# Layer-norm sums S1 to S4 moved from VectorE to GpSimd in a two-layer graph network kernel

## The chip, the cores and the metric

The kernel runs on one core of one Trainium2 chip. Five engines work side by side on it: TensorE (PE, matrix products), VectorE (DVE, elementwise), ScalarE (ACT, activations and copies), GpSimd (POOL, elementwise, slower) and SyncE (SP, which here issues DMAs). The metric is the device time of one execution in microseconds (us); the time before is 1575.23 us, the median of 3 runs (1575.11 to 1575.33).

## What is computed

```
# layer 0
h = relu(layernorm(x))                      # x: (16, 1024, 128)
x = x + (adj @ (h @ W0) + b0)               # adj: (1024, 1024)
# layer 1, five gated steps
h = relu(layernorm(x))
repeat 5 times:
    m  = adj @ h ; av = [m, m]
    z  = sigmoid(av @ w3.T + w3_b + h @ u3.T + u3_b)
    r  = sigmoid(av @ w4.T + w4_b + h @ u3.T + u3_b)
    hv = tanh(av @ w5.T + w5_b + (r * h) @ u5.T + u5_b)
    h  = (1 - z) * h + z * hv
x = x + h
```

## The kernel before

The 16 batches go in 4 groups `p` of 4 batches, each group in two slots of 2 batches. A group takes two layer rounds (`layer(p, slot)`: adj times the normalised x, layer 0) and ten step rounds (`step(p, t, slot)`: the five gated steps of layer 1). `all_rounds` gives the order, the same on every engine: the layer rounds of group p+1 are put among the last step rounds of group p, and the two slots alternate, so that TensorE works on one slot while the other engines finish the other.

adj times h is done by a Strassen-like scheme of seven half-size products (K_A0, K_S1, K_S2, K_A1, K_S3, K_B1, K_S4) with fp16 high and low parts, so each product is 12 matmuls of 128x512. Four of the seven need sums of the quarters of h. For the state inside a step they are made by `sum_state` on VectorE. For a layer norm's output they are the subject here:

- `moments` (L322 to L349, GpSimd): 18 small instructions on 128x16 that turn the statistics into `rstd` and `shift`.
- `normalise` (L810, ScalarE): writes the normalised rows into the one buffer `ysc`, 4 quarters of 4 blocks.
- `round_n` part 0 and 1 (L826, ScalarE) and `rest_n` part 0 and 1 (L1190, VectorE): the fp16 high and low parts of the four plain quarters.
- `sum_n` (L1201, L1202, L1205, L1207, VectorE): four adds and subtractions of 128x512 fp32 that overwrite `ysc` by S1 to S4. They wait for the low parts 0 and 1 of `rest_n`, since those read what is overwritten. Its `parts` let the caller put two of the four in each of two places.
- `round_n` and `rest_n` part 2 and 3: the high and low parts of S1 to S4. Part 2 (S1, S2) waits for the third of the four instructions, part 3 for the fourth. K_S1 to K_S4 of TensorE wait for these.

There are 16 such layer norms: (p, layer, slot). Layer 0 of a group is normalised while the group before still steps; layer 1 between the group's layer rounds and its first steps. Each engine executes its instructions strictly in the order in which its function writes them; semaphores (`wait_ge`) tie the engines together. What comes just behind the sums matters in three places: `new_state` (L1232, L1236, L1238, VectorE) makes the new h of the other slot, whose completion (`h_ready`) ScalarE's `evacuate` (L850) waits for, and TensorE cannot open the bank of K_S2 before that evacuation. `output` (L1284) adds the result to x.

The two lines that decide who waits for a sum:

```
act.wait_ge(n_sum_done[layer], 4 * n + part + 1)   # round_n, part 2 and 3
pool.wait_ge / dve.wait_ge(n_lo_done[layer], 4 * n + 2)   # first sum
```

Of the kernel before, what the change touches and what calls it, by code (L numbers as in the profile page):

```python
# [5 lines left out]
def gnn_kernel(nc, x, adj, w0, b0, w3, b3, u3, c3, w4, b4, w5, b5, u5, c5, out):  # L6
# [13 lines left out]
    END = STEPS - 1  # L20
# [42 lines left out]
    with ctx:  # L63
# [70 lines left out]
        ysc = sb("ysc", [P, 2 * BLOCKS, D])  # L134
# [149 lines left out]
        def n_layer(p, slot):  # L284
            return 2 * p + slot
# [199 lines left out]
        @block.gpsimd  # L485
        def _(pool):
            pool.memset(ones[:, :], 1.0)
            pool.memset(ident[:, :], 0.0).then_inc(ident_done, 1)
            pool.wait_ge(ident_done, 1)
            pool.affine_select(out=ident[:, :], in_=ident[:, :], compare_op=ALU.not_equal, fill=1.0, base=0,  # L490
                               pattern=[[-1, P]], channel_multiplier=1).then_inc(ident_done, 1)

            def scale_weights():


                pool.wait_ge(top_ready, 1)
                pool.wait_ge(w_maxed, 1)
                nc.gpsimd.tensor_scalar(w_max[:, 3:5], w_max[:, 3:5], 1.0 / SCALE16, None, ALU.mult)
                nc.gpsimd.tensor_scalar(w_max[:, 0:3], w_max[:, 0:3], m_inv[:, :], 1.0, ALU.mult, ALU.mult
                                        ).then_inc(w_op, 1)  # L500
                pool.wait_ge(w_op, 1)
                nc.gpsimd.tensor_scalar(w_max[:, 1:2], w_max[:, 1:2], w_max[:, 0:1], None, ALU.max)
                nc.gpsimd.tensor_scalar(w_max[:, 2:3], w_max[:, 2:3], w_max[:, 4:5], None, ALU.max
                                        ).then_inc(w_op, 1)
                pool.wait_ge(w_op, 2)
                nc.gpsimd.tensor_scalar(w_max[:, 1:2], w_max[:, 1:2], w_max[:, 3:4], None, ALU.max).then_inc(w_op, 1)
                pool.wait_ge(w_op, 3)
                nc.gpsimd.tensor_scalar(w_exp[:, :], w_max[:, 1:3].bitcast(I32), 1.0 / EXP_UNIT, LEAST_EXP,
                                        ALU.mult, ALU.max).then_inc(w_op, 1)
                pool.wait_ge(w_op, 4)  # L510
                nc.gpsimd.tensor_scalar(w_scale[:, :].bitcast(I32), w_exp[:, :], -EXP_UNIT,
                                        (254 + TOP_EXP) * EXP_UNIT, ALU.mult, ALU.add)
                nc.gpsimd.tensor_scalar(w_inv[:, :].bitcast(I32), w_exp[:, :], EXP_UNIT, -TOP_EXP * EXP_UNIT,
                                        ALU.mult, ALU.add).then_inc(w_op, 1)
                pool.wait_ge(w_op, 5)
                for w, by, also in ((WZR, GATES, m_inv[:, :]), (WR, GATES, m_inv[:, :]), (WV, CAND, m_inv[:, :]),
                                    (UZR, GATES, 1.0 / SCALE16), (UV, CAND, 1.0 / SCALE16)):
                    last = nc.gpsimd.tensor_scalar(w_raw[:, w, :], w_raw[:, w, :], w_scale[:, by:by + 1], also,
                                                   ALU.mult, ALU.mult)
                last.then_inc(w_scaled, 1)  # L520

            for slot in range(2):
                moments(pool, 0, 0, slot)
            scale_weights()
            for slot in range(2):
                moments(pool, 0, 1, slot)
            for p in range(1, GROUPS):
                for layer in range(2):
                    for slot in range(2):
                        moments(pool, p, layer, slot)  # L530

        @block.tensor
        def _(pe):
# [520 lines left out]
        def _(dve):  # L1054
# [135 lines left out]
                nc.vector.tensor_sub(lo8[:, at[1], :], rows4[:, at[0], :], hi8[:, at[1], :]  # L1190
                                     ).then_inc(n_lo_done[layer], 1)

            def sum_n(p, layer, slot, parts=range(2)):

                n, done = n_layer(p, slot), n_sum_done[layer]
                a0, a1, b0_, b1 = (flat(quarter(ysc, q)) for q in range(4))
                if 0 in parts:
                    dve.wait_ge(n_lo_done[layer], 4 * n + 2)
                    if layer == 0:
                        dve.wait_ge(y_ready[0], 4 * n + 4)  # L1200
                    nc.vector.tensor_add(b1, b0_, b1).then_inc(done, 1)  # L1201
                    nc.vector.tensor_sub(b0_, a0, b0_).then_inc(done, 1)  # L1202
                if 1 in parts:
                    dve.wait_ge(done, 4 * n + 1)
                    nc.vector.tensor_sub(a0, b1, a0).then_inc(done, 1)  # L1205
                    dve.wait_ge(done, 4 * n + 3)
                    nc.vector.tensor_sub(a1, a1, a0).then_inc(done, 1)  # L1207

            def first_h(p, slot):
                for k in range(2):  # L1210
                    part = (slice(None), slice(2 * k, 2 * k + 2), slice(None))
# [75 lines left out]
            def layer(p, slot):  # L1287
                g = g_layer(p, slot)
                if p == 0 and slot == 0:
# [5 lines left out]
                    rest_n(0, 0, 0, 0)  # L1295
                    rest_n(0, 0, 0, 1)
                    rest_rows(K_A1)
                    sum_n(0, 0, 0)
                    sum_rows(K_S2)
                    rest_rows(K_S4)  # L1300
                    rest_n(0, 0, 0, 2)
# [14 lines left out]
                    rest_m(g, 3)  # L1316
                    rest_m(g, 2)
                    rest_n(0, 0, 1, 1)
                    sum_n(0, 0, 1)
                    sum_m(g, 1, START_ORDER)  # L1320
                    rest_n(0, 0, 1, 2)
                    rest_m(g, 1)
# [3 lines left out]
                elif p == 0:  # L1326
# [8 lines left out]
                    rest_m(g, 2)  # L1335
                    sum_m(g, 1, LAYER_ORDER)
                    rest_m(g, 1)
                    sum_n(0, 1, 0)
                    rest_n(0, 1, 0, 2)
                else:  # L1340
                    t, other = (END, 0) if slot == 1 else (END - 1, 1)
# [27 lines left out]
            def step(p, t, slot):  # L1369
# [39 lines left out]
                if sums:  # L1409
                    rest_s(e, 1)  # L1410
                rest_m(g, 3)
                if steps_ahead(p, t, slot, END, 0):
                    sum_n(p + 1, 0, 1, [0])
                rest_m(g, 2)
                if t == 0:
                    dve.wait_ge(h_first_done, 2 * n_layer(p, slot) + 2)
# [7 lines left out]
                sum_m(g, 1)  # L1424
                rest_rh(s, 3)
                rest_m(g, 1)
                if steps_ahead(p, t, slot, END, 0):
                    sum_n(p + 1, 0, 1, [1])
                if steps_ahead(p, t, slot, 3, 0):
                    rest_n(p + 1, 0, 0, 0)  # L1430
                if steps_ahead(p, t, slot, END, 1):
                    rest_n(p + 1, 1, 0, 1)
                    sum_n(p + 1, 1, 0, [0])
                if steps_ahead(p, t, slot, 3, 1):
                    sum_n(p + 1, 0, 0, [1])
                times_h(s, slot, 2)
                if first0 and p > 0:
                    rest_n(p, 1, 1, 1)
                times_h(s, slot, 1)
                rest_rh(s, 2)  # L1440
                if first0 and p > 0:
                    sum_n(p, 1, 1, [0])
                rest_rh(s, 1)
                if first0 and p > 0:
                    sum_n(p, 1, 1, [1])
                if steps_ahead(p, t, slot, END, 1):
                    sum_n(p + 1, 1, 0, [1])
                    rest_n(p + 1, 1, 0, 2)
                    rest_n(p + 1, 1, 0, 3)
                if steps_ahead(p, t, slot, 1, 1):  # L1450
# [2 lines left out]
                    statistics0(p + 1, 1)  # L1453
                if steps_ahead(p, t, slot, 3, 0):
                    rest_n(p + 1, 0, 0, 1)
                    sum_n(p + 1, 0, 0, [0])
                if steps_ahead(p, t, slot, 3, 1):
                    rest_n(p + 1, 0, 0, 2)
                    rest_n(p + 1, 0, 0, 3)
# [8 lines left out]
                if first0 and p == 0:  # L1468
                    rest_n(p, 1, 1, 0)
                    rest_n(p, 1, 1, 1)  # L1470
                    sum_n(p, 1, 1)

            all_rounds(layer, step)
            s, n = n_step(GROUPS - 1, END, 1), n_layer(GROUPS - 1, 1)
# [31 lines left out]
```

## Time and profile before

| | |
|---|---|
| median of 3 runs | 1575.23 us |
| the profiled execution | 1574.88 us |
| its span, first to last instruction | 1573.1 us |
| TensorE busy | 1464.5 us, 93% |
| VectorE busy | 1256.9 us, 80% |
| ScalarE busy | 948.5 us, 60% |
| GpSimd busy | 169.8 us, 11% |
| mean granted TensorE clock | 0.976 of full speed (2.4 GHz) |

The profile is of one execution. Between the span and the execution's own time lie 1.8 us of launch and end. A row of a timeline has the start, the duration, the engine, the line, the operation and the shapes; in brackets stands how long the engine was idle before and what released it. "x2" is two instructions merged in one row. TensorE's matmuls overlap, so that a row of one shows 0.38 us while twelve take 2.59 us.

### The profile page before, as it was taken

What the parts mean: (1) busy time and instruction counts of PE and PEld (TensorE: products, weight loads), DVE (VectorE), ACT (ScalarE), POOL (GpSimd) and SP (SyncE); (2) the same over time, 40 slices, a digit from 0 to 9 for tenths busy, and PEclk for the clock granted to TensorE, in tenths of its full rate; (3) what the DMA queues carried; (4) which work ended last, traced back from release to release, by engine and by line L of the source; (5) the groups of instructions that cost most, each with busy time, mean ns of one, the idle gap of its engine ahead of it and who ended that gap; (6) DMA issues with size and microseconds to landing.
All of it is one profiled execution on the core that took longest, in us unless ns stands there. A gap on an engine that the chain in (4) does not pass through costs nothing.

```text
span 1573.1 us, 19899 instructions
## 1 busy us (share of the span) xinstructions
PE 1464.5 (93%) x6951; PEld 673.5 (43%) x6951; DVE 1256.9 (80%) x1697; ACT 948.5 (60%) x1470; POOL 169.8 (11%) x388
## 2 busy tenths in 40 slices
PE   4778999999998899999998999999999889999997
PEld 3433444444443344444443434444444334444443
DVE  8866888888857978988877878888885787887777
ACT  5536566766546665676564755676664656556653
POOL 1212004400210001500101000440021000000000
PEclk9889999999999999999999999999999999999998
DMA  4011334321213243333212234422221323333322
GB/s 177 1 27 27 78 61 94 58 54 41 48 31 78 57 91 101 57 69 62 38 24 67 57 75 87 94 57 54 41 48 31 77 54 64 78 57 64 67 49 80
DMA packets 316625, 97.42 MB, mean 62 GB/s; under 512 B 310256, under 2 KB 311152, under 8 KB 316528
## 3 DMA queue, kind: packets, MB, share of 16 engines
q1 hardware_dynamic: 314800, 95.49, 28.3%
q8 instruction: 57, 0.93, 0.3%
q10 hardware_dynamic: 1728, 0.66, 0.2%
q14 instruction: 40, 0.33, 0.1%
HBM read 13.24 MB, written 8.39 MB: 14 GB/s over the span
## 4 chain that ended last, share of the span: by engine, by line
PE 77%; DVE 12%; ACT 5%; issue 4%; POOL 1%; DMA 1%; ACTq 0%; SPq 0%; DVEq 0%; POOLq 0%
PE ps_a L562 29%; PE ps_c L562 13%; PE ps_b L562 7%; PE ps_u L618 6%; PE ps_u L622 6%; PE ps_u L620 6%; PE ps_v L620 4%; PE ps_v L622 4%; PE ps_v L618 4%; DVE nx_lo L1190 2%; ACT ysc L810 1%; DVE t_lo L1111 1%; ACT nx_hi L826 1%; DVE rh L1236 1%; DVE area L1238 1%
## 5 line engine op out<-in xcount | busy, mean ns | idle before, releaser
L562 PE MATMUL ps_a<-t_hi,nx_hi 128*128 128x512 f16 x640 | 248.8, 389 | 47.1 <-ACT rh L850 19.8
L562 PE MATMUL ps_a<-t_lo,nx_hi 128*128 128x512 f16 x640 | 248.6, 388 | 0.0
L562 PE MATMUL ps_a<-t_hi,nx_lo 128*128 128x512 f16 x640 | 248.1, 388 | 0.0
L850 ACT ACTIVATE rh<-ps_a 128x512 f32<-128x512 f32 x144 | 85.1, 591 | 197.7 <-PE ps_a L562 161.1
L863 ACT ACTIVATE rh<-ps_v,bias,w_inv 128x512 f32<-128x512 f32 x160 | 123.8, 776 | 93.0 <-PE ps_v L622 93.0
L1271 DVE TENSOR_TENSOR rh<-rh,area 128x512 f32<-128x512 f32 x160 | 108.9, 691 | 65.8 <-ACT rh L868 62.0
L859 ACT ACTIVATE m_hi<-rh 128x512 f16<-128x512 f32 x144 | 90.1, 627 | 112.2 <-DVE rh L1221 111.7
L1226 DVE SCALAR_TENSOR_TENSOR m_lo<-rh,m_hi 128x512 f16<-128x512 f32 x144 | 99.0, 691 | 56.7 <-ACT m_hi L859 51.3
L1232 DVE SCALAR_TENSOR_TENSOR rh<-rh,area 128x1024 f32<-128x1024 f32 x80 | 97.8, 1222 | 44.7 <-ACT rh L863 44.3
L876 ACT ACTIVATE area<-ps_u,bias,w_inv 128x512 f32<-128x512 f32 x160 | 122.4, 771 | 17.2 <-PE ps_u L622 16.9
L868 ACT ACTIVATE rh<-ps_u,bias,w_inv 128x512 f32<-128x512 f32 x160 | 120.0, 774 | 17.6 <-PE ps_u L622 16.0
L1275 DVE TENSOR_TENSOR rh_lo<-rh,rh_hi 128x512 f16<-128x512 f32 x160 | 110.0, 687 | 25.0 <-ACT rh_hi L881 23.4
L322 POOL TENSOR_TENSOR mean<-stats 128x16 f32<-128x16 f32 x16 | 15.8, 988 | 1008.0 <-DVE stats L1149 516.3
L618 PE MATMUL ps_u<-m_hi,w_hi 128*128 128x512 f16 x320 | 121.5, 380 | 0.4
L622 PE MATMUL ps_u<-m_hi,w_lo 128*128 128x512 f16 x320 | 121.5, 380 | 0.0
L620 PE MATMUL ps_u<-m_lo,w_hi 128*128 128x512 f16 x320 | 121.5, 380 | 0.0
L562 PE MATMUL ps_c<-t_lo,nx_hi 128*128 128x512 f16 x320 | 121.3, 379 | 0.0
L562 PE MATMUL ps_c<-t_hi,nx_lo 128*128 128x512 f16 x320 | 121.3, 379 | 0.0
L562 PE MATMUL ps_c<-t_hi,nx_hi 128*128 128x512 f16 x320 | 121.3, 379 | 0.0
L562 PEld LDWEIGHTS ps_a<-t_hi,nx_hi 128*128 128x128 f16 x640 | 63.6, 99 | 131.6 <-issue 25.8
L830 ACT ACTIVATE h_hi<-area 128x1024 f16<-128x1024 f32 x78 | 82.2, 1054 | 58.6 <-DVE area L1238 58.6
L1236 DVE TENSOR_TENSOR rh<-rh,area 128x1024 f32<-128x1024 f32 x80 | 98.3, 1228 | 8.7 <-DVE rh L1232 0.5
(180 smaller groups left out, 3053.3 us busy)
## 6 DMA issues: line engine op xcount, KB each, us to landing
xr<-in_x_dram SPq DMA_DIRECT2D x6, 1024.0 KB, 5.1
out_dram<-xr SPq DMA_DIRECT2D x6, 1024.0 KB, 4.0
area<-in_adj_dram SPq DMA_DIRECT2D x8, 512.0 KB, 8.3
nx_hi<-s SPq DMA_TRANSPOSE x128, 2.4
nx_lo<-s SPq DMA_TRANSPOSE x128, 2.5
area<-in_x_dram SPq DMA_DIRECT2D x2, 1024.0 KB, 5.1
nx_hi<-h_hi SPq DMA_TRANSPOSE x96, 2.4
nx_lo<-h_lo SPq DMA_TRANSPOSE x96, 2.5
```

The costliest lines, as they stand in the source:

```text
L562: last = nc.tensor.matmul(o[:, :], a[:, PLACE[k], j, :], b[:, k, j, :], start=(opens and j == 0 and n == 0), stop=(j == HB - 1 and n == 2) ...
L618: nc.tensor.matmul(bank_out[:, :], w_hi[:, w, :], a_hi[:, q, :], start=start, stop=False, skip_group_check=reopen)
L620: nc.tensor.matmul(bank_out[:, :], w_hi[:, w, :], a_lo[:, q, :], start=False, stop=False, skip_group_check=reopen)
L622: return nc.tensor.matmul(bank_out[:, :], w_lo[:, w, :], a_hi[:, q, :], start=False, stop=stop, skip_group_check=reopen)
L863: nc.scalar.activation(cand[:, q, :], V_BANK[q][:, :], ACT.Tanh, bias=bias[:, BV:BV + 1], scale=w_inv[:, CAND:CAND + 1]).then_inc(cand_rea ...
L868: nc.scalar.activation(rh[:, q, :], U_BANK[q][:, :], ACT.Sigmoid, bias=bias[:, BR:BR + 1], scale=w_inv[:, GATES:GATES + 1]).then_inc(r_rea ...
L876: nc.scalar.activation(z[:, q, :], U_BANK[q][:, :], ACT.Sigmoid, bias=bias[:, BZ:BZ + 1], scale=w_inv[:, GATES:GATES + 1]).then_inc(z_read ...
L1226: nc.vector.scalar_tensor_tensor(out=m_lo[:, q, :], in0=source, scalar=M_SCALE, in1=m_hi[:, q, :], op0=ALU.mult, op1=ALU.subtract).then_in ...
L1232: nc.vector.scalar_tensor_tensor(out=cand[part], in0=cand[part], scalar=SCALE16, in1=h[slot][part], op0=ALU.mult, op1=ALU.subtract).then_i ...
L1236: nc.vector.tensor_mul(cand[part], cand[part], z[part]).then_inc(zdiff_done, 1)
L1271: nc.vector.tensor_mul(rh[:, q, :], rh[:, q, :], h[slot][:, q, :]).then_inc(rh_done, 1)
L1275: nc.vector.tensor_sub(rh_lo[:, q, :], rh[:, q, :], rh_hi[:, q, :]).then_inc(rh_lo_done, 1)
```

## The change

`sum_n` is taken out of VectorE's program with all its calls, and written as a function of GpSimd's, with the same four instructions, waits and semaphore counts. GpSimd calls it between its `moments`: right behind the moments of the same norm at the start (group 0), and in the groups 1 to 3 as follows: the moments of both slots of layer 0, the sums (0, slot 0), the moments (1, slot 0), the sums (0, slot 1), the moments (1, slot 1), and then the sums of layer 1 of both slots. The split of the four instructions over two places is gone. TensorE's, ScalarE's and SyncE's programs stay as they are.

```diff
@@ gpsimd
-            for slot in range(2):
-                moments(pool, 0, 0, slot)
+            def sum_n(p, layer, slot):
+
+                n, done = n_layer(p, slot), n_sum_done[layer]
+                a0, a1, b0_, b1 = (flat(quarter(ysc, q)) for q in range(4))
+                pool.wait_ge(n_lo_done[layer], 4 * n + 2)
+                if layer == 0:
+                    pool.wait_ge(y_ready[0], 4 * n + 4)
+                nc.gpsimd.tensor_add(b1, b0_, b1).then_inc(done, 1)
+                nc.gpsimd.tensor_sub(b0_, a0, b0_).then_inc(done, 1)
+                pool.wait_ge(done, 4 * n + 1)
+                nc.gpsimd.tensor_sub(a0, b1, a0).then_inc(done, 1)
+                pool.wait_ge(done, 4 * n + 3)
+                nc.gpsimd.tensor_sub(a1, a1, a0).then_inc(done, 1)
+
+            moments(pool, 0, 0, 0)
+            sum_n(0, 0, 0)
+            moments(pool, 0, 0, 1)
             scale_weights()
-            for slot in range(2):
-                moments(pool, 0, 1, slot)
+            sum_n(0, 0, 1)
+            moments(pool, 0, 1, 0)
+            sum_n(0, 1, 0)
+            moments(pool, 0, 1, 1)
+            sum_n(0, 1, 1)
             for p in range(1, GROUPS):
-                for layer in range(2):
-                    for slot in range(2):
-                        moments(pool, p, layer, slot)
+                for slot in range(2):
+                    moments(pool, p, 0, slot)
+                sum_n(p, 0, 0)
+                moments(pool, p, 1, 0)
+                sum_n(p, 0, 1)
+                moments(pool, p, 1, 1)
+                for slot in range(2):
+                    sum_n(p, 1, slot)
@@ vector
-            def sum_n(p, layer, slot, parts=range(2)):
...
@@ vector, the calls (each removed)
-                if steps_ahead(p, t, slot, END, 0):
-                    sum_n(p + 1, 0, 1, [0])
...
-                    sum_n(p + 1, 1, 0, [0])
...
-                    sum_n(p, 1, 1)
```

What moves is shown by the order of the instructions at two places. The first is GpSimd in group 1, behind the moments of layer 1, slot 1 (L345 to L349 end the moments, `ysc` is the buffer of the sums). Before:

```order
L345 TENSOR_SCALAR newton<-newton 128x16
L347 TENSOR_TENSOR rstd<-rstd,newton 128x16
L349 TENSOR_TENSOR shift<-mean,rstd 128x16
L322 TENSOR_TENSOR mean<-stats 128x16
L323 TENSOR_TENSOR gap<-stats 128x16
```

And now:

```order
L345 TENSOR_SCALAR newton<-newton 128x16
L347 TENSOR_TENSOR rstd<-rstd,newton 128x16
L349 TENSOR_TENSOR shift<-mean,rstd 128x16
L529 TENSOR_TENSOR ysc<-ysc 128x512
L530 TENSOR_TENSOR ysc<-ysc 128x512
L532 TENSOR_TENSOR ysc<-ysc 128x512
L534 TENSOR_TENSOR ysc<-ysc 128x512
L529 TENSOR_TENSOR ysc<-ysc 128x512
L530 TENSOR_TENSOR ysc<-ysc 128x512
L532 TENSOR_TENSOR ysc<-ysc 128x512
L534 TENSOR_TENSOR ysc<-ysc 128x512
```

Eight large instructions stand behind the last moments of the group, those of slot 0 and of slot 1.

The second is VectorE in the first step round of group 1, where the sums of layer 1, slot 1 were (`nx_lo` are the low parts, `rh` the product of r and h, L1232 begins the new state). Before:

```order
L1271 TENSOR_TENSOR rh<-rh,area 128x512
L1190 TENSOR_TENSOR nx_lo<-ysc,nx_hi 128x1024
L1271 TENSOR_TENSOR rh<-rh,area 128x512
L1275 TENSOR_TENSOR rh_lo<-rh,rh_hi 128x512
L1201 TENSOR_TENSOR ysc<-ysc 128x512
L1202 TENSOR_TENSOR ysc<-ysc 128x512
L1275 TENSOR_TENSOR rh_lo<-rh,rh_hi 128x512
L1205 TENSOR_TENSOR ysc<-ysc 128x512
L1207 TENSOR_TENSOR ysc<-ysc 128x512
L1190 TENSOR_TENSOR nx_lo<-ysc,nx_hi 128x2x512
L1232 SCALAR_TENSOR_TENSOR rh<-rh,area 128x2x512
```

And now (the same functions, 23 lines further down until the removed `sum_n`, 7 behind it):

```order
L1278 TENSOR_TENSOR rh<-rh,area 128x512
L1213 TENSOR_TENSOR nx_lo<-ysc,nx_hi 128x1024
L1278 TENSOR_TENSOR rh<-rh,area 128x512
L1282 TENSOR_TENSOR rh_lo<-rh,rh_hi 128x512 x2
L1213 TENSOR_TENSOR nx_lo<-ysc,nx_hi 128x2x512
L1239 SCALAR_TENSOR_TENSOR rh<-rh,area 128x2x512
```

The four rows on `ysc` are gone; the low part of S1 and S2 still stands in front of the new state.

## Rows read from the trace of the kernel before

**Rows 1.** Page, part 1: busy time of each engine.
```profile
PE 1464.5 (93%) x6951; PEld 673.5 (43%) x6951; DVE 1256.9 (80%) x1697; ACT 948.5 (60%) x1470; POOL 169.8 (11%) x388
```

**Rows 2.** Page, part 4: the chain that ended last, by engine.
```profile
PE 77%; DVE 12%; ACT 5%; issue 4%; POOL 1%; DMA 1%; ACTq 0%; SPq 0%; DVEq 0%; POOLq 0%
```

**Rows 3.** Waits of TensorE: waiter, releaser, us in total, times, longest.
```profile
PE ps_a L562 <- DVE nx_lo L1190: 18.2, 5, 3.7
PE ps_a L562 <- DVE ny_lo L1190: 8.5, 3, 2.8
```

**Rows 4.** Tile ysc: one of the four sums; min/median/max ns.
```profile
L1201 DVE TENSOR_TENSOR ysc<-ysc x16: 683/692/707, 30.1 to 1267.8; 128x512 f32<-128x512 f32 x16
```

**Rows 5.** GpSimd's groups by shape: count, busy us, mean ns.
```profile
L518 POOL TENSOR_SCALAR nx_hi<-nx_hi,w_scale,m_inv 128x128 f32<-128x128 f32 x3 | 1.3, 451 | 0.1
L518 POOL TENSOR_SCALAR nx_hi<-nx_hi,w_scale 128x128 f32<-128x128 f32 x2 | 0.7, 370 | 0.0
```

**Rows 6.** Timeline, GpSimd beside VectorE, then (457.99) GpSimd alone.
```profile
281.52 1.26 DVE L1236 TENSOR_TENSOR rh<-rh,area 128x1024 f32<-128x1024 f32 x1
...
281.66 1.21 POOL L324 TENSOR_TENSOR var_eps<-stats 128x16 f32<-128x16 f32 x1
...
457.99 0.23 POOL L324 TENSOR_TENSOR var_eps<-stats 128x16 f32<-128x16 f32 x1
```

**Rows 7.** Timeline 339 to 348 us: sums of group 1, layer 0, slot 0.
```profile
339.28 0.69 DVE L1190 TENSOR_TENSOR ny_lo<-ysc,ny_hi 128x512 f16<-128x512 f32 x1
...
341.41 1.23 DVE L1232 SCALAR_TENSOR_TENSOR rh<-rh,area 128x1024 f32<-128x1024 f32 x1
...
344.00 1.22 DVE L1238 TENSOR_TENSOR area<-area,rh 128x1024 f32<-128x1024 f32 x1
...
345.79 0.59 ACT L850 ACTIVATE rh<-ps_a 128x512 f32<-128x512 f32 x1
...
347.50 0.38 PE L562 MATMUL ps_a<-t_hi,nx_hi 128*128 128x512 f16 x1
```

**Rows 8.** Timeline 415 to 423 us: group 1, layer 0, slot 1.
```profile
415.97 0.69 POOL L349 TENSOR_TENSOR shift<-mean,rstd 128x16 f32<-128x16 f32 x1
...
421.60 1.04 ACT L826 ACTIVATE ny_hi<-ysc 128x1024 f16<-128x1024 f32 x1
```

**Rows 9.** Timeline 474 to 482 us: group 1, layer 1, slot 0.
```profile
474.34 1.22 DVE L1190 TENSOR_TENSOR nx_lo<-ysc,nx_hi 128x1024 f16<-128x1024 f32 x1
...
480.70 1.06 ACT L826 ACTIVATE nx_hi<-ysc 128x1024 f16<-128x1024 f32 x1 [1.36 <-DVE ysc L1205]
```

**Rows 10.** Timeline 517 to 525 us: group 1, layer 1, slot 1.
```profile
517.32 1.23 DVE L1190 TENSOR_TENSOR nx_lo<-ysc,nx_hi 128x1024 f16<-128x1024 f32 x1 [0.25 <-ACT nx_hi L826]
...
522.46 1.05 ACT L826 ACTIVATE nx_hi<-ysc 128x1024 f16<-128x1024 f32 x1
...
523.55 1.23 DVE L1190 TENSOR_TENSOR nx_lo<-ysc,nx_hi 128x1024 f16<-128x1024 f32 x1 [0.46 <-ACT nx_hi L826]
```

**Rows 11.** Timeline 25 to 35 us: group 0, layer 0, slot 0.
```profile
25.73 1.83 DVE L1190 TENSOR_TENSOR ny_lo<-ysc,ny_hi 128x1024 f16<-128x1024 f32 x2
...
32.64 2.28 DVE L1098 TENSOR_TENSOR s<-area 128x2048 f32<-128x2048 f32 x1
```

**Rows 12.** Timeline 70 to 75 us: group 0, layer 0, slot 1.
```profile
70.74 0.68 DVE L1190 TENSOR_TENSOR ny_lo<-ysc,ny_hi 128x512 f16<-128x512 f32 x1
...
73.39 1.06 ACT L826 ACTIVATE ny_hi<-ysc 128x1024 f16<-128x1024 f32 x1 [2.77 <-DVE ysc L1205]
```

**Rows 13.** Timeline 101 to 111 us: group 0, layer 1, slot 0.
```profile
101.89 2.36 DVE L1190 TENSOR_TENSOR nx_lo<-ysc,nx_hi 128x1024 f16<-128x1024 f32 x2 [8.36 <-ACT nx_hi L826]
...
108.68 2.00 ACT L826 ACTIVATE nx_hi<-ysc 128x1024 f16<-128x1024 f32 x2 [2.56 <-DVE ysc L1205]
```

**Rows 14.** Timeline 146 to 152 us: group 0, layer 1, slot 1.
```profile
146.00 2.36 DVE L1190 TENSOR_TENSOR nx_lo<-ysc,nx_hi 128x1024 f16<-128x1024 f32 x2 [1.58 <-ACT nx_hi L826]
...
150.32 1.06 ACT L826 ACTIVATE nx_hi<-ysc 128x1024 f16<-128x1024 f32 x1 [2.74 <-DVE ysc L1205]
```

More of the change, by code:

```diff
@@ L1191, in rest_n @@
                                      ).then_inc(n_lo_done[layer], 1)
-            def sum_n(p, layer, slot, parts=range(2)):
[L1195 to L1207, printed above, removed]
             def first_h(p, slot):
@@ L1297, in layer @@
                     rest_rows(K_A1)
-                    sum_n(0, 0, 0)
                     sum_rows(K_S2)
@@ L1318, in layer @@
                     rest_n(0, 0, 1, 1)
-                    sum_n(0, 0, 1)
                     sum_m(g, 1, START_ORDER)
@@ L1337, in layer @@
                     rest_m(g, 1)
-                    sum_n(0, 1, 0)
                     rest_n(0, 1, 0, 2)
@@ L1426, in step @@
                 rest_m(g, 1)
-                if steps_ahead(p, t, slot, END, 0):
-                    sum_n(p + 1, 0, 1, [1])
                 if steps_ahead(p, t, slot, 3, 0):
@@ L1432, in step @@
                     rest_n(p + 1, 1, 0, 1)
-                    sum_n(p + 1, 1, 0, [0])
-                if steps_ahead(p, t, slot, 3, 1):
-                    sum_n(p + 1, 0, 0, [1])
                 times_h(s, slot, 2)
@@ L1440, in step @@
                 rest_rh(s, 2)
-                if first0 and p > 0:
-                    sum_n(p, 1, 1, [0])
                 rest_rh(s, 1)
-                if first0 and p > 0:
-                    sum_n(p, 1, 1, [1])
                 if steps_ahead(p, t, slot, END, 1):
-                    sum_n(p + 1, 1, 0, [1])
                     rest_n(p + 1, 1, 0, 2)
@@ L1455, in step @@
                     rest_n(p + 1, 0, 0, 1)
-                    sum_n(p + 1, 0, 0, [0])
                 if steps_ahead(p, t, slot, 3, 1):
```

## Prediction

> **What bounds the kernel now.** I read the busy times first, then the chain of work that ended last, then who TensorE waited for, then the 16 places of the sums one by one. TensorE is busy for 93% of the span, VectorE for 80%, GpSimd for 11% [rows 1]: GpSimd has room, and VectorE is not the bound on average. The chain agrees: 77% of it lies on TensorE, 12% on VectorE, 5% on ScalarE [rows 2]. So 64 instructions less on VectorE are worth nothing where TensorE runs on. They matter where TensorE waits, and there the rows name layer-norm low parts: 18.2 us in 5 waits for `nx_lo` and 8.5 us in 3 waits for `ny_lo` [rows 3]. These stand behind the sums in the dependences (copy of S1 and S2, then low part, then on VectorE the new state). What counts is therefore not the time that a sum takes of an engine, but when its third instruction ends, and what it keeps VectorE from.
>
> **What is removed.** 64 sums of 0.69 us [rows 4], at most 44 us of VectorE in all, 2.8 us per norm. Waits, matmuls, copies and DMAs are as before; no DMA moves past another queue.
>
> **What is added: the price of a sum on GpSimd.** The trace has none of this size. GpSimd's nearest rows are scalings of 128x128, 0.44 us each in the form with two pointers (1.3 us for 3) and 0.36 with one (0.7 us for 2) [rows 5], against 0.23 us for a 128x16 instruction alone [rows 6]. The slopes are 0.13/112 = 1.2 ns and 0.21/112 = 1.9 ns per element; 496 elements more give 0.8 and 1.15 us. In proportion to elements alone the dear form gives 4 x 0.44 = 1.75 us. A sum reads two tensors, so I take the dearer form's slope, 1.15 us, and keep 0.8 and 1.75 as ends. The Trainium skill (GPSIMD Engine Reference, "Performance versus the Vector engine") measures 4497 ns for a two-input add of 2048 elements, an estimate of about 1.12 us for 512, by which the sum below would be the same.
>
> **What the two engines do to each other.** A 128x16 instruction on GpSimd takes 0.23 us alone but 1.21 us when it starts 0.14 us behind VectorE's L1236, and it ends 0.09 us after that one's end (281.66 + 1.21 = 282.87 against 281.52 + 1.26 = 282.78) [rows 6]. So GpSimd waits for the end of a VectorE instruction with two SBUF inputs. For the other direction the rows show only a trace: that L1236 takes 1.26 us, where its like of the same size, L1232, takes 1.23 [rows 6, 7]. A sum has 32 times the elements of that GpSimd instruction, 32 x 0.03 = 1.0 us: I take it that VectorE stands still for about 1.05 us per sum whenever it wants to start an instruction with two SBUF inputs meanwhile, and that they then take turns. The ends are 0 (nothing held) and 1.75 (the sum's whole length at its dear price). The Trainium skill (SBUF — State Buffer, "Who interferes with whom") says that the two share a read port, exclusively and for a whole instruction. Taken literally it makes the hold the full length of the sum, 1.15 us, and would add 0.1 us to each hold.
>
> **Group 0 (all four norms lie on the chain).**
> - Layer 0, slot 0: GpSimd can begin when the low parts end, 27.56. VectorE next does high and low parts of adj out of PSUM, which read one SBUF tensor, and then L1098, which before began at 32.64 behind the sums [rows 11] and could now where the first sum began, 30.1 [rows 4]. GpSimd's third sum holds it to about 31.1. VectorE has no idle time from there until the next norm's statistics: -1.5.
> - Layer 0, slot 1: the low part ends at 71.42, three sums later it is 71.42 + 3 x 1.15 + 0.1 = 74.97; ScalarE's copy, which waits for them, began at 73.39 [rows 12] and everything queued behind it goes with it: +1.55.
> - Layer 1, slot 0: from 104.25 three sums end at 107.8, or 108.4 with one VectorE instruction in between, against 108.68 [rows 13]: -0.3.
> - Layer 1, slot 1: from 148.36, ready at 151.9 against 150.32 [rows 14]; nothing else is left for VectorE to do there: +1.55.
>
> Together +1.3 us.
>
> **Groups 1 to 3 (three times the same picture, 374 us apart).**
> - Layer 0, slot 0: the low part ends at 339.97, and GpSimd runs its four sums from there, long before the copy that needs them. From 341.41 VectorE makes the new state: three dependent instructions with two SBUF inputs each, up to L1238 (344.00) [rows 7]. The second sum has just begun when L1232 wants to start, the third and fourth get in at its two next boundaries: 1.0 + 1.05 + 1.05 = 3.1 us later. Cover: L1238 ended at 345.22, the evacuation L850 began at 345.79 (0.57 us of slack), ended at 346.38, and TensorE needed it at 347.50 (1.12 us) [rows 7]. So TensorE waits 3.1 - 0.57 - 1.12 = 1.4, say 1.5 us with the semaphores, in a stretch where it has no idle time: +1.5. The two sums that VectorE is spared further on give nothing back, for TensorE doesn't wait there.
> - Layer 0, slot 1: GpSimd's moments end at 416.66, and its sums are queued behind them (before, two of them ran on VectorE earlier than that). The third ends at 416.66 + 3 x 1.15 = 420.1 plus two or three turns of VectorE of 0.69, 421.5 or 422.2; the copy began at 421.60 [rows 8]. VectorE's small work shifts by up to 1 us, but TensorE's wait of 2.8 us behind it hangs on a later evacuation and the fourth sum, long ready: 0.
> - Layer 1, slot 0: from 475.56, three sums and three turns of VectorE: 475.56 + 3.45 + 2.07 = 481.08, against 480.70 for a copy that waited 1.36 us for a sum already [rows 9]. What VectorE is spared it spends on being held: +0.4.
> - Layer 1, slot 1: the low part ends at 518.55. Three sums and three turns (one `rh`, two `rh_lo`): 518.55 + 3.45 + 2.07 = 524.07. The copy began at 522.46, its low part at 523.55, and the new state, on which TensorE's 3.7 us wait hangs, directly behind [rows 10, 3]: 524.07 - 522.46 = +1.6.
>
> Together 3.5 us per group, 10.5 for three. Behind the waiting sums on GpSimd stand only moments whose statistics come later than the sums end, so nothing else is held up.
>
> **Sum.** 1.3 + 10.5 = +11.8 us. The profiled execution took 1574.88 us, so 1586.7; the median of the runs is 0.35 above it: 1587.0 us.
>
> **The rivals.**
> 1. *VectorE is not held by GpSimd* (other side). Only GpSimd gives way. Then group 0 comes to -2.5 (L1098 at 30.1 instead of 32.64) + 1.55 - 0.9 (107.8 against 108.68) + 1.55 = -0.3 us; in the later groups the first and last places cost nothing and at 480.70 the copy comes when ScalarE is free, 1.36 us earlier [rows 9]: -1.4 x 3 = -4.2, in all -4.5 us, 1571 us. For it speaks that VectorE's row is longer by 0.03 us only; against it, that it is longer at all. It decides if the hold is under about 0.2 us.
> 2. *Short sums.* At 0.8 to 0.9 us per sum each third sum ends 0.9 us earlier: 3 x 0.9 + 0.3 less in group 0, about 0.75 less in each of the three costly places of the others, 9.8 in all: +2.0 us, 1577 us, which no measurement of this kernel tells from no change (0.2%, 3.2 us, is the bound used below).
> 3. *Long sums*, 1.75 us: 0.6 x 3 = 1.8 us more at each of three places in group 0 and 0.6 at the first, 1.8 more at each of the four of the other groups: 6 + 21.6 more, 1615 us.
> 4. *The change does nothing* is no case: the order of GpSimd and VectorE moves as written, and the ends of the sums move with it.
>
> **How the numbers follow.** The forecast has 0.52, rival 1 0.15, rival 2 0.18, rival 3 0.10; 0.05 is left for a mix that lands near zero or just below. The range 1570 to 1600 takes in the forecast with holds of 0.8 to 1.4 us and rivals 1 and 2, and leaves rival 3 out. Slower by over 0.2%: 0.52 + 0.10 + a little of rival 2 = 0.65; within: 0.18; faster: 0.17.
>
> **What would show it.** Right: GpSimd's sums of 1.1 to 1.2 us alone and 1.7 to 1.9 beside VectorE; L1232 to L1238 of the place at 341 us, or those between them, longer by about 1 us each or started that much later; TensorE idle by 1 to 2 us before K_S2 at 347 us; the copy at 522.46 released by a GpSimd sum. Wrong: VectorE rows of unchanged length beside the sums, or TensorE's waits for `nx_lo` shorter than 18.2 us in all.

## The result and the profile after

| | before | after |
|---|---|---|
| median of the runs (range) | 1575.28 us (1575.11 to 1577.5), 4 runs | 1590.42 us (1589.21 to 1591.99), 4 runs |
| profiled execution | 1574.88 us, span 1573.1 | 1591.56 us, span 1589.8 |
| granted TensorE clock, mean over the span | 0.976 | 0.973 |

The ratio is 1.0096, with a 95% interval of 1.008 to 1.0111: the change costs 15.1 us (12.6 to 17.5). The forecast was 11.8 us.

The page's busy times and its chain by engine, of the changed kernel:

```profile
PE 1473.5 (93%) x6951; PEld 675.3 (42%) x6951; DVE 1255.0 (79%) x1633; ACT 949.2 (60%) x1470; POOL 264.7 (17%) x452
...
PE 75%; DVE 12%; ACT 5%; issue 4%; POOL 3%; DMA 0%; ACTq 0%; SPq 0%; DVEq 0%; POOLq 0%
```

Against [rows 1] VectorE has 64 instructions less, which were 44 us of work [rows 4], and yet is only 1.9 us less busy (1256.9 to 1255.0). The other 42 us came back as longer instructions. GpSimd went from 1% of the chain [rows 2] to 3%.

The four sums on GpSimd, by tile (count, then min/median/max ns, first and last start):

```profile
L529 POOL TENSOR_TENSOR ysc<-ysc x16: 1264/1270/1657, 27.7 to 1282.0; 128x512 f32<-128x512 f32 x16
L530 POOL TENSOR_TENSOR ysc<-ysc x16: 1263/1714/1733, 28.9 to 1283.2; 128x512 f32<-128x512 f32 x16
L532 POOL TENSOR_TENSOR ysc<-ysc x16: 1267/1718/3434, 30.1 to 1284.9; 128x512 f32<-128x512 f32 x16
```

A sum takes 1.27 us when nothing is in its way and mostly 1.72 us beside VectorE; one took 3.43. The prediction had 1.15 alone and expected 1.7 to 1.9 beside VectorE.

VectorE beside GpSimd, in the timeline of group 1 (start us, length us; in brackets the idle time before and its releaser). This is the place of [rows 7], layer 0, slot 0; the kernel's lines have moved, L1232 is L1239, L1236 is L1243, L1238 is L1245, L850 is L873 and L562 is L585:

```profile
344.55 1.27 POOL L529 TENSOR_TENSOR ysc<-ysc 128x512 f32<-128x512 f32 x1 [41.87 <-DVE ny_lo L1213]
345.77 1.27 POOL L530 TENSOR_TENSOR ysc<-ysc 128x512 f32<-128x512 f32 x1
345.92 2.20 DVE L1239 SCALAR_TENSOR_TENSOR rh<-rh,area 128x1024 f32<-128x1024 f32 x1 [1.45 <-ACT rh L886]
347.00 2.25 POOL L532 TENSOR_TENSOR ysc<-ysc 128x512 f32<-128x512 f32 x1
348.22 2.10 DVE L1243 TENSOR_TENSOR rh<-rh,area 128x1024 f32<-128x1024 f32 x1
...
350.36 2.17 DVE L1245 TENSOR_TENSOR area<-area,rh 128x1024 f32<-128x1024 f32 x1
...
353.27 0.39 PE L585 MATMUL ps_a<-t_hi,nx_hi 128*128 128x512 f16 x1 [1.10 <-ACT rh L873]
```

The engines take turns, one instruction each. L1239 starts 0.15 us behind the second sum and needs 1.23 us alone [rows 7]; the sum ends at 345.77 + 1.27 = 347.04, and 347.04 + 1.23 = 348.27 against its end at 348.12, 0.15 us earlier. The third sum, issued at 347.00, ends 1.13 us behind that, at 349.25. Each of the three VectorE instructions is 0.87 to 0.97 us longer than in [rows 7] (L1236 there takes 1.23 us). At the end of them stands a TensorE wait of 1.10 us where none was. The Trainium skill (SBUF — State Buffer, "Who interferes with whom") says that the port pair which VectorE and GpSimd share is an exclusive lock, and that a VectorE instruction with two SBUF inputs contends with a GpSimd instruction that reads SBUF; these rows agree, in both directions.

### The profile page after: what moved, and what is told of

Read it like the earlier page. It is cut to its first block, busy times and chain, and to the rows that moved or that the text cites. A ratio compares the mean times of both kernels' runs of the same rounds, so it can differ in the third digit from the quotient of the medians.

```text
span 1589.8 us, 19899 instructions
## 1 busy us (share of the span) xinstructions
PE 1473.5 (93%) x6951; PEld 675.3 (42%) x6951; DVE 1255.0 (79%) x1633; ACT 949.2 (60%) x1470; POOL 264.7 (17%) x452
## 4 chain that ended last, share of the span: by engine, by line
PE 75%; DVE 12%; ACT 5%; issue 4%; POOL 3%; DMA 0%; ACTq 0%; SPq 0%; DVEq 0%; POOLq 0%
PE ps_a L585 29%; PE ps_c L585 12%; PE ps_b L585 7%; PE ps_u L641 5%; PE ps_u L643 5%; PE ps_u L645 5%; PE ps_v L643 3%; PE ps_v L641 3%; PE ps_v L645 3%; DVE nx_lo L1213 2%; DVE area L1245 1%; DVE rh L1243 1%; DVE rh L1239 1%; ACT nx_hi L849 1%; DVE t_lo L1134 1%
## 5 line engine op out<-in xcount | busy, mean ns | idle before, releaser
L585 PE MATMUL ps_a<-t_hi,nx_hi 128*128 128x512 f16 x640 | 250.3, 391 | 53.6 <-ACT rh L873 28.0
L585 PE MATMUL ps_a<-t_lo,nx_hi 128*128 128x512 f16 x640 | 249.7, 390 | 0.0
L585 PE MATMUL ps_a<-t_hi,nx_lo 128*128 128x512 f16 x640 | 249.4, 390 | 0.0
L873 ACT ACTIVATE rh<-ps_a 128x512 f32<-128x512 f32 x144 | 85.2, 592 | 215.7 <-PE ps_a L585 166.3
L1278 DVE TENSOR_TENSOR rh<-rh,area 128x512 f32<-128x512 f32 x160 | 119.6, 756 | 71.0 <-ACT rh L891 66.4
L1233 DVE SCALAR_TENSOR_TENSOR m_lo<-rh,m_hi 128x512 f16<-128x512 f32 x144 | 102.5, 716 | 59.1 <-ACT m_hi L882 54.1
L1282 DVE TENSOR_TENSOR rh_lo<-rh,rh_hi 128x512 f16<-128x512 f32 x160 | 123.6, 775 | 21.7 <-ACT rh_hi L904 20.4
L1239 DVE SCALAR_TENSOR_TENSOR rh<-rh,area 128x1024 f32<-128x1024 f32 x80 | 100.6, 1258 | 45.3 <-ACT rh L886 45.1
L585 PEld LDWEIGHTS ps_a<-t_hi,nx_hi 128*128 128x128 f16 x640 | 63.9, 100 | 140.0 <-ACT rh L873 34.4
L585 PE MATMUL ps_c<-t_hi,nx_hi 128*128 128x512 f16 x320 | 121.3, 379 | 0.7 <-DVE nx_lo L1213 0.7
L585 PE MATMUL ps_c<-t_hi,nx_lo 128*128 128x512 f16 x320 | 121.3, 379 | 0.0
L585 PE MATMUL ps_c<-t_lo,nx_hi 128*128 128x512 f16 x320 | 121.3, 379 | 0.0
L1243 DVE TENSOR_TENSOR rh<-rh,area 128x1024 f32<-128x1024 f32 x80 | 100.9, 1261 | 8.3
```

The costliest lines, as they stand in the source:

```text
L585: last = nc.tensor.matmul(o[:, :], a[:, PLACE[k], j, :], b[:, k, j, :], start=(opens and j == 0 and n == 0), stop=(j == HB - 1 and n == 2) ...
L1233: nc.vector.scalar_tensor_tensor(out=m_lo[:, q, :], in0=source, scalar=M_SCALE, in1=m_hi[:, q, :], op0=ALU.mult, op1=ALU.subtract).then_in ...
L1239: nc.vector.scalar_tensor_tensor(out=cand[part], in0=cand[part], scalar=SCALE16, in1=h[slot][part], op0=ALU.mult, op1=ALU.subtract).then_i ...
L1243: nc.vector.tensor_mul(cand[part], cand[part], z[part]).then_inc(zdiff_done, 1)
L1278: nc.vector.tensor_mul(rh[:, q, :], rh[:, q, :], h[slot][:, q, :]).then_inc(rh_done, 1)
L1282: nc.vector.tensor_sub(rh_lo[:, q, :], rh[:, q, :], rh_hi[:, q, :]).then_inc(rh_lo_done, 1)
```

## Where the time went

TensorE's waits for the same three releasers, of the changed kernel (us in total, times, longest). Before, the first was 19.8 us in 10 waits, the others are [rows 3]:

```profile
PE ps_a L585 <- ACT rh L873: 28.0, 13, 5.5
PE ps_a L585 <- DVE nx_lo L1213: 18.5, 5, 3.7
PE ps_a L585 <- DVE ny_lo L1213: 8.5, 3, 2.8
...
PE ps_u L641 <- DVE m_lo L1233: 1.3, 3, 0.4
```

The waits for low parts, 26.7 us before and 27.0 now, did not change. Three new ones of 1.1 us (layer 0, slot 0), three grown from 0.38 to 1.56 (layer 1, slot 1) and three of 0.44 us for `m_lo` (layer 0, slot 1) make 3 x (1.10 + 1.18 + 0.44) = 8.2 us for groups 1 to 3. Of the first row another 1.4 us belong to group 0: experiment 10, which changes that group alone, has 21.2 us there.

That is not the whole of it. I split each span in three by 2 us windows of TensorE's rows: idle time; time lost to a low clock while busy (busy time x (1 - granted clock), full being 2.4 GHz and 0.50 being 1.2 GHz); and the rest, work at full speed. The last two together are the page's busy time: 1464.5 us before and 1473.5 after, for the same 6951 matmuls.

| profiled execution | span | TensorE idle | lost to low clock | work at full speed |
|---|---|---|---|---|
| before | 1573.1 | 108.6 | 24.8 | 1439.7 |
| after | 1589.8 | 116.3 | 32.7 | 1440.8 |
| difference | +16.7 | +7.7 | +7.9 | +1.1 |

About half of the 16.7 us is clock. The clearest place is behind group 0. Both kernels wait 3.72 us there for a low part; the matmul behind the wait, before and after:

```profile
166.17 0.38 PE L562 MATMUL ps_a<-t_hi,nx_hi 128*128 128x512 f16 x1 [3.72 <-DVE nx_lo L1190]
```

```profile
167.77 0.59 PE L585 MATMUL ps_a<-t_hi,nx_hi 128*128 128x512 f16 x1 [3.72 <-DVE nx_lo L1213]
```

And TensorE in the windows behind it (window, its length, TensorE's busy us with its matmuls, granted clock, DMA share, GB/s), before:

```profile
168.00:170.00 2.00, 2.00 (x11) 1.00 0.00 0
170.00:172.00 2.00, 2.00 (x11) 1.00 0.32 66
```

After:

```profile
168.00:170.00 2.00, 2.00 (x6) 0.50 0.03 8
170.00:172.00 2.00, 2.00 (x7) 0.50 0.00 0
172.00:174.00 2.00, 2.00 (x7) 0.58 0.32 66
```

After a wait of the same length the old kernel went on at full clock and the new one at half for 6 us, which costs 2 x 0.50 x 2 + 2 x 0.42 = 2.8 us, more than any two of the new waits. The same happened behind the waits at 545.6 and 821.9 us (before, 538.3 and 810.7), 1.6 and 1.7 us. The second of them is a wait of 2.82 us in both kernels; after:

```profile
821.91 0.38 PE L585 MATMUL ps_a<-t_hi,ny_hi 128*128 128x512 f16 x1 [2.82 <-DVE ny_lo L1213]
...
822.00:824.00 2.00, 2.00 (x6) 0.55 0.00 0
```

In groups 1 to 3 no low stretch stands behind one of the new waits. In the profiles of both kernels and of every experiment they lie (taken as 2 us windows with a granted clock under 0.95) at three old waits of each group: the one of 3.7 us where the group before ends, the one of 2.8 us some 275 us later, and the one of 5.5 us some 330 us later. At the third the clock fell every time. Behind the other two it fell at 3 of 6 places before and at 6 of 6 after.

Group by group, from the starts of the same matmuls before and after:

| matmul before | after | difference | forecast at that point |
|---|---|---|---|
| 64.74 | 62.16 | -2.6 | -1.5 |
| 104.91 | 104.38 | -0.5 | about 0 |
| 166.17 (end of group 0) | 167.77 | +1.6 | +1.3 |
| 538.31 (end of group 1) | 545.63 | +7.3 | +4.8 |
| 910.15 (end of group 2) | 924.17 | +14.0 | +8.3 |
| 1286.21 (end of group 3) | 1302.90 | +16.7 | +11.8 |

The same groups with idle time and low clock apart, beside two experiments told below that leave the program of groups 1 to 3 as it was (length, in brackets idle / lost to low clock, us):

| | before | experiment 1 | experiment 10 | after |
|---|---|---|---|---|
| group 0 | 166.2 (51.8 / 9.0) | 165.1 (49.8 / 9.8) | 168.2 (51.0 / 11.6) | 167.8 (51.4 / 11.3) |
| group 1 | 372.1 (14.5 / 3.8) | 375.5 (14.5 / 7.4) | 373.2 (14.5 / 5.0) | 377.9 (17.3 / 6.4) |
| group 2 | 371.8 (15.3 / 2.5) | 376.1 (15.3 / 6.6) | 371.9 (15.3 / 2.4) | 378.5 (18.2 / 5.7) |
| group 3 | 376.1 (15.7 / 6.2) | 371.8 (15.3 / 2.6) | 371.9 (15.3 / 2.6) | 378.7 (18.2 / 5.9) |

The new waits of groups 1 to 3 are all there: idle time grows by 8.2 us, as counted above. But a group whose program and waits are the same takes anything from 371.8 to 376.1 us, by the clock: its idle time differs by 0.4 us at most. The kernel before has one such dear group in its profile, the changed one has three.

## The experiments

Two theories stood at the start, here with the letters that the expectations give them. **A**: GpSimd's two-input sums and VectorE's two-input instructions exclude each other, the time is the waits that this makes, and it adds up place by place. **C**: VectorE is not held, only GpSimd gives way; the time comes from sums that are late in themselves. The expectations also weigh **B**: any sum on GpSimd costs, wherever it stands. As the clock rows came in, **D** was added: beside its waits the change makes TensorE's clock fall more often.

All kernels start from the one before. In most of them a set says which sums go to GpSimd, each at the place in GpSimd's order that the change gives it; the others stay on VectorE as before:

```diff
+    ON_POOL = {(0, 0, 0)}          (group, layer, slot)
@@ sum_n of GpSimd (the added one) @@
+                if (p, layer, slot) not in ON_POOL:
+                    return
@@ sum_n of VectorE (the old one) @@
+                if (p, layer, slot) in ON_POOL:
+                    return
```

**1. Only the first norm** (`ON_POOL = {(0, 0, 0)}`).

> Only the very first norm's sums (group 0, layer 0, slot 0) are made by GpSimd, the other 15 stay on VectorE. Theory A (a sum costs by when its third instruction ends and by what it holds up on VectorE): this is the one place of the 16 where it gains, since VectorE is dense there and most of its neighbours read PSUM; TensorE's product at 64.7 us starts 2.5 us earlier (62.2 in the changed kernel) and the time falls by 2 to 3 us. Theory B (any sum on GpSimd costs): slower by 1 us or more. The adj-row sum L1098 starts at 30.1 instead of 32.6 by A.

Measured: 1574.58 us (12 runs, 1569.73 to 1578.38) against 1576.18 (19 runs), ratio 0.9987 with 0.9973 to 1.0001. In the profile TensorE's idle time is 2.5 us less, 106.1. The place of [rows 11]:

```profile
30.31 3.44 POOL L535 TENSOR_TENSOR ysc<-ysc 128x512 f32<-128x512 f32 x1
...
30.33 2.28 DVE L1124 TENSOR_TENSOR s<-area 128x2048 f32<-128x2048 f32 x1
```

L1124 (L1098 before) came through unheld at its old 2.28 us, and the third sum waited for it, 3.44 us, where nothing hurries it. TensorE's product comes at 62.52 us instead of 64.74, 2.2 us earlier. That the kernel is faster isn't shown, since the interval reaches 1.0001, but the 1 us or more that B asks for is excluded. In its profile the loss to low clock is 6.1 us larger (30.9), more than the wait gave, and most of that lies in groups 1 and 2, whose program is the old one (table above).

**2. Only layer 0, slot 0 of groups 1 to 3** (`ON_POOL = {(p, 0, 0) for p in (1, 2, 3)}`).

> Only the sums of layer 0, slot 0 in groups 1 to 3 are made by GpSimd. Nobody waits for these sums for 25 us, so all they can do is stand in VectorE's way. Theory A (both engines hold each other for a whole instruction): TensorE waits 1.1 us before K_S2 three times, +3.3 us, and if the low TensorE clock behind pauses differs between kernels, up to +6 us more. Theory C (only GpSimd gives way): no TensorE wait there, 0.

Measured: 1581.29 us (5 runs), ratio 1.003 with 1.0018 to 1.0042, +5.1 us by the medians. The new wait stands in each group:

```profile
352.56 0.39 PE L588 MATMUL ps_a<-t_hi,nx_hi 128*128 128x512 f16 x1 [1.11 <-ACT rh L876]
```

Three such waits are 3.3 us. They support A against C: these sums end long before their reader needs them, so only the holding of VectorE can cost here.

**3. Only layer 1, slot 1 of groups 1 to 3** (`ON_POOL = {(p, 1, 1) for p in (1, 2, 3)}`).

> Only the sums of layer 1, slot 1 in groups 1 to 3 are made by GpSimd. Theory A: the third sum ends 1.2 to 1.5 us after the moment at which ScalarE was ready for it, TensorE's wait of 0.4 us before K_S2 becomes 1.6 us three times, +3.6 us; with a clock effect +3.6 to +9. Theory C: 3 x 0.7 us at most, since the sums alone take 3 x 1.27 us from the low part on.

Measured: 1583.27 us (8 runs), ratio 1.0039 with 1.0026 to 1.0052. The wait behind the new state is 1.56 us where it was 0.38 before, in all three groups, as in the full change. That is 3.5 us of waits for a difference of 7.1 us.

**4. The two middle norms of groups 1 to 3** (`ON_POOL = {(p, 0, 1), (p, 1, 0) for p in (1, 2, 3)}`).

> Only the sums (layer 0, slot 1) and (layer 1, slot 0) of groups 1 to 3 are made by GpSimd. Theory A: the first costs 0.45 us of TensorE's wait for m_lo, the second about 0.1 us: +1.6 us in all, with no low-clock stretch more than before. Theory B (any sum on GpSimd costs 0.5 us or more per norm): +3 us or more.

Measured: 1581.65 us (5 runs), ratio 1.0043 with 1.003 to 1.0055, +6.7 us. The new waits are three for `m_lo`, 1.6 us in all, as expected, and one old wait of 3.7 us is 4.1 long; the longest of the new ones:

```profile
799.19 0.38 PE L644 MATMUL ps_u<-m_hi,w_hi 128*128 128x512 f16 x1 [0.73 <-DVE m_lo L1254]
```

TensorE's idle time over the whole span is no longer than before (108.3 against 108.6), but its loss to low clock is 31.5, 6.7 more. The expectation by A, +1.6 us with no more low clock, was missed, and the time itself is the +3 us or more of B. The waits alone can't explain this run; D can.

**5. The full change, with the sums of layer 0, slot 0 held back** until the new state is done:

```diff
                 if layer == 0:
                     pool.wait_ge(y_ready[0], 4 * n + 4)
+                if p > 0 and layer == 0 and slot == 0:
+                    pool.wait_ge(c_done, 3 * g_step(p - 1, END - 1, 1) + 2)
```

> All 16 sums on GpSimd as in the changed kernel, but those of layer 0, slot 0 in groups 1 to 3 wait until VectorE has made the new state and the sum m of quarter 3 of that round (some 12 us later, still 10 us before their reader). Theory A: TensorE's three waits of 1.1 us go, -3.3 us against the changed kernel (1590.4), to about 1587; if the low clock goes with them, to 1583. Theory C or one in which only the third sum's end counts: no change, 1590.

Measured: 1590.46 us (4 runs), ratio 1.0091 with 1.0078 to 1.0104: not faster than the change. The wait of 1.10 us is gone, and two others stand in its place, 0.90 us here and 0.89 us at 371.46:

```profile
361.81 2.08 POOL L534 TENSOR_TENSOR ysc<-ysc 128x512 f32<-128x512 f32 x1 [59.92 <-DVE rh L1251]
...
362.69 1.76 DVE L1256 SCALAR_TENSOR_TENSOR m_lo<-rh,m_hi 128x512 f16<-128x512 f32 x1
...
364.59 0.38 PE L646 MATMUL ps_u<-m_hi,w_hi 128*128 128x512 f16 x1 [0.90 <-DVE m_lo L1256]
364.97 2.83 DVE L1301 TENSOR_TENSOR rh<-rh,area 128x512 f32<-128x512 f32 x2
```

`m_lo` takes 1.76 us instead of 0.69. The number alone is also what C had expected; the rows decide. The expectation by A took the later stretch for a free one; TensorE hangs on VectorE there just as closely.

**6. Before, with four two-input GpSimd instructions beside the new state**; their results are not used.

```diff
+            def beside(p):
+                pool.wait_ge(n_sum_done[0], 4 * n_layer(p, 0) + 2)
+                for k in range(4):
+                    nc.gpsimd.tensor_sub(scratch[:, :], t_hi[:, K_A0, 0, :], t_hi[:, K_A0, 1, :]).then_inc(beside_op, 1)
+                    pool.wait_ge(beside_op, 4 * (p - 1) + k + 1)
```

> The kernel before, all sums on VectorE, with four additional GpSimd instructions per group 1 to 3 at about 341 us in each group: tensor_sub of 128x512 that reads two fp16 blocks of a finished table and writes an unused buffer, one after the other, beside the new state. Their result is not used. Theory A: each holds VectorE's L1232, L1236, L1238 for about 1 us; h_ready 3 us later, TensorE waits 1 to 1.5 us, +3 to +4.5 us in all. Theory C (VectorE isn't held): 0. The three VectorE instructions show durations of 2 us and more by A, 1.22 by C.

Measured: 1589.8 us (4 runs) against 1574.93 (15 runs), ratio 1.0094 with 1.0081 to 1.0108. All sums are on VectorE as before, and yet:

```profile
344.99 7.43 POOL L544 TENSOR_TENSOR top_diag<-t_hi 128x512 f16<-128x512 f16 x4 [43.20 <-DVE ysc L1239]
345.03 2.19 DVE L1269 SCALAR_TENSOR_TENSOR rh<-rh,area 128x1024 f32<-128x1024 f32 x1
...
347.33 1.99 DVE L1273 TENSOR_TENSOR rh<-rh,area 128x1024 f32<-128x1024 f32 x1
```

C falls: GpSimd instructions on which nothing depends make VectorE's 1.23 us instructions 2.0 to 2.2 us long. The size was missed widely. The profile has 3.5 us more idle time of TensorE, as expected, and 11.7 us more busy time for the same matmuls (1476.2). The column of low clock has 13.9 us more (38.7), but 4.7 of them lie in the first 65 us, which took only 0.1 us longer than before. Twelve instructions that no one waits for cost as much as the whole change.

**7. The same with eight memsets of the same tile**, which write it and read nothing; unused as well.

```diff
+                for k in range(8):
+                    nc.gpsimd.memset(scratch[:, :], 0.0).then_inc(beside_op, 1)
+                    pool.wait_ge(beside_op, 8 * (p - 1) + k + 1)
```

> As beside_read, but the additional GpSimd instructions are eight memsets of 128x512 fp16 per group, which read nothing. If VectorE is held by GpSimd's reads of SBUF only, nothing changes: 0 us and VectorE's rows of 1.22 us. If any GpSimd instruction holds it, +1 us or more per group as in beside_read.

Measured: 1576.09 us (11 runs), ratio 1.0005 with 0.9996 to 1.0014, no difference.

```profile
341.54 4.60 POOL L544 MEMSET top_diag<- 128x512 f16 x8 [43.19 <-DVE ysc L1239]
...
341.60 1.22 DVE L1269 SCALAR_TENSOR_TENSOR rh<-rh,area 128x1024 f32<-128x1024 f32 x1
```

VectorE is at its old 1.22 us right beside GpSimd's memsets. So it isn't GpSimd's being busy that holds it, nor its writing to SBUF; what is left is its reading. Its loss to low clock stayed too (25.0).

**8 and 9. Before and after once more.** They show how far one profiled execution can be trusted.

> The kernel before, unchanged, profiled once more. In its profile TensorE lost 24.8 us to the low clock while busy and was idle for 108.5. If the low-clock stretches follow from the kernel's pauses alone, both numbers come again within 1 us; if they fall by chance, the idle time comes again and the loss differs by 2 to 8 us.

> The changed kernel, profiled once more: idle 115.5 us and 32.7 us lost to the low clock in its first profile. By chance: idle the same, the loss anywhere between 25 and 35. By the kernel: the same loss within 1 us.

Measured: 1575.20 and 1590.35 us. The expectations have the idle time of the first profiles as 108.5 and 115.5 us; over the whole span it is 108.6 and 116.3. It repeats to 0.2 us (108.4 and 116.4); the loss to low clock is 25.4 and 35.4, where the first profiles had 24.8 and 32.7. The kernel before thus repeated within 1 us, group by group too, and the changed one did not. So the added clock loss is 7.9 us in one pair and 10.0 in the other; but 4.3 us of the second pair's lie in the first 62.2 us, which took as long in both profiles of the changed kernel. By TensorE's busy time the pairs have 9.0 and 7.2 us. One pair of profiles could be chance; the times say that it isn't all chance: the slowest of 23 runs of the kernel before took 1578.46 us, with the 7.7 us of idle time 1586.2, and the fastest of five of the changed one took 1589.21.

**10. Only group 0, all four norms** (`ON_POOL` = those with p = 0).

> Only the four norms of group 0 have their sums made by GpSimd. Theory A with the measured lengths (1.27 us a sum alone, the third ready 3.75 us after the low part): -2.6 at the first norm, +2.0 at the second, +0.2 at the third, +1.7 at the fourth, +1.3 us by 168 us, and nothing behind it. The forecast's terms for the same places were -1.5, +1.55, -0.3 and +1.55.

Measured: 1579.42 us (12 runs) against 1575.71 (23 runs), ratio 1.0015 with 1.0005 to 1.0026. The twelve runs lie in two heaps, three at 1574.4 to 1574.9 and nine at 1579.1 to 1580.5, with the same program. The profiled one is of the lower heap (span 1573.0, loss 25.9), though its group 0 ends later than before's, at 168.24 instead of 166.17. Group 0's steps are -2.2, +2.0 and +2.3 us (by 62.5, 104.7 and 168.2 us), where the expectation adds up to -2.6, +2.0 and +1.9; behind it the idle time is the old one, as expected, and group 3 takes 371.9 us instead of 376.1. That the heaps lie 5 us apart fits D, since one group's clock makes 4.3 us, but no profile of the upper heap was taken, and the mean clock on record for each run doesn't separate them cleanly (0.974 to 0.977 in the lower, 0.968 to 0.974 in the upper).

**11. Only the fourth sum of all 16 norms on GpSimd**; sums 1 to 3 stay on VectorE.

```diff
+                pool.wait_ge(done, 4 * n + 3)
+                nc.gpsimd.tensor_sub(a1, a1, a0).then_inc(done, 1)
@@ sum_n of VectorE @@
-                    dve.wait_ge(done, 4 * n + 3)
-                    nc.vector.tensor_sub(a1, a1, a0).then_inc(done, 1)
```

> VectorE makes the first three sums of every norm where it did, GpSimd the fourth alone, which is read last: no reader waits longer for its sum, VectorE is spared 16 x 0.69 = 11 us and can be held once per norm for 1.2 us instead of four times. Theory A: within 2 us of the kernel before, no TensorE wait longer than before except by a few tenths. Theory B (any sum on GpSimd costs): +3 us or more.

Measured: 1577.08 us (12 runs), ratio 1.0012 with 1.0002 to 1.0022. TensorE idles 2.9 us less (105.7), and 4.1 us more go to low clock (28.9). The +1.4 us by the medians are within the 2 us of A; the 3 us of B lie above them, but within the interval (0.3 to 3.5 us). No version that ran is shown to beat the kernel before.

The parts of the change by medians, +3.7 (group 0), +5.1, +7.1 and +6.7 us, make 22.6, the whole is 15.1: the waits add up, the clock doesn't. In groups 1 to 3 idle time grows by 3.3, 3.2 and 1.4 us in experiments 2, 3 and 4, 7.9 together against 8.2 in the full change. Where low clock falls just ahead of a wait, the wait also gets shorter, so that over a whole span idle time and busy time trade with each other by a few us.

## Why the prediction was right, and where it wasn't

- **Direction and mechanism: right.** Two-input instructions of the two engines take turns (experiments 6 and 7), VectorE is held, and the places named are where TensorE waits. Rival 1 (VectorE not held, 1571 us) fell with experiment 6 and the rows of L1239, L1243 and L1245.
- **Price of a sum: 1.27 us, taken as 1.15**, from a slope over rows of 128x128. Rivals 2 (0.8 to 0.9 us) and 3 (1.75) are out. The Trainium skill (GPSIMD Engine Reference, "Performance versus the Vector engine") has 4497 ns for 2048 elements; a quarter of it, the estimate of 1.12 us, is 0.15 us below what this trace has.
- **Group 0, layer 0, slot 0: -1.5 taken, -2.6 measured.** I let the third sum hold L1098 for 1 us. In the trace the two start within 0.02 us of each other and the sum paid (3.43 us); VectorE began 2.5 us earlier and unheld, as in rival 1.
- **Group 0 in all: +1.3 taken, +1.6 measured, in part by luck.** The two steps of +1.55 are there and larger: the copy of layer 0, slot 1, which had waited 2.77 us [rows 12], waits 4.64, and that of layer 1, slot 1, which had waited 2.74 us [rows 14], waits 4.61, 1.9 more each. The larger gain at the first norm hides that. And of TensorE's time in group 0 it is the low clock that grew, by 2.3 us, not the idle time (0.4 less).
- **Layer 0, slot 0 of groups 1 to 3: +1.5 taken, 1.10 measured.** The hold came to 0.97 + 0.87 + 0.95 = 2.8 us instead of 3.1.
- **Layer 0, slot 1: 0 taken, 0.44 measured.** I called VectorE's small work free to shift by 1 us. It wasn't: `m_lo` at 423.04 took 1.75 us, and TensorE hung on it.
- **Layer 1, slot 0: +0.4 taken, about 0.1 measured.** The copy did wait longer, 2.16 us instead of 1.36 [rows 9], but behind that stood slack.
- **Layer 1, slot 1: +1.6 taken, 1.56 - 0.38 = 1.2 measured**; the copy is now released by a GpSimd sum, as said:

```profile
526.46 3.44 DVE L1282 TENSOR_TENSOR rh_lo<-rh,rh_hi 128x512 f16<-128x512 f32 x2
...
529.38 1.06 ACT L849 ACTIVATE nx_hi<-ysc 128x1024 f16<-128x1024 f32 x1 [0.17 <-POOL ysc L532]
```

The waits of groups 1 to 3 were thus 8.2 us instead of 10.5. Had they been all, the kernel would have come out at 1575.2 + 1.6 + 8.2 = 1585.

**The step that failed is a term left out.** The sum treated TensorE's speed as given: it priced waits and nothing behind them. In the profile 7.9 of 16.7 us are time lost to half clock, most of it in stretches that the old kernel ran at full clock behind equal waits. The total of 15.1 against 11.8 is therefore closer than the reasoning deserves: waits too dear by 4.1 us (11.8 against 7.7 of idle time), and 7.9 us of clock not seen. That the two misses partly cancel is luck.

**What stays open.** Which pauses of TensorE are followed by low clock. Behind 3.72 us at the end of group 0 the clock fell in one kernel and not in the other. Experiments 4 and 6 show that TensorE can be busy for 8.1 and 11.7 us more with no new wait over 0.9 us, experiment 1 that the clock of groups 1 and 2 can change with their program unchanged, and experiment 10 that one program can end 5 us apart. The places are known, two old waits in each group, but not what decides between full and half clock there: it may be the moment at which the pause comes, or TensorE's work ahead of it, and no run isolates either.

## What to carry to other kernels

- An instruction moved to GpSimd does not free VectorE when it reads two SBUF tensors: 44 us of sums moved, 1.9 us of busy time saved. Price each as a hold of VectorE of nearly its own length wherever VectorE wants an instruction with two SBUF inputs, and put it only where VectorE idles, or reads one input from PSUM (L1228, 686 ns beside the sums as before).
- Before you move work off the engine that looks loaded, ask who waits for its last result and when: taking 44 us of sums off VectorE left TensorE's 26.7 us of waits for low parts as they were (27.0).
- In a kernel with TensorE at 93%, account for idle time and low clock apart. Here the low clock lay behind old waits and not behind the new ones, and came and went with edits far from it, so that the parts of a change didn't add up.

## What the runs showed of the hardware that I had not expected

- Half clock behind a pause is not a matter of its length alone: 3.72 us with and without it, at the same place of the program. A stretch costs 1.2 to 2.9 us, and all of them, by the windows, 24.8 to 38.7 us per execution.
- Twelve GpSimd instructions whose results no one uses cost 14.9 us of 1575.
- Who goes first isn't settled by the recorded starts. At 30.1 us the two started within 0.02 us and VectorE ran unheld, while the sum, recorded as the first, took 3.43 us. At 526.46 two small VectorE instructions beside sums took 3.44 us instead of 1.4.
